# Local-attention layers on one core: the block transposes of the weights move ahead of the sums of squares on VectorE

## The reference

```
qkv = shift(x) @ Wqkv                        # half of the channels come from the token before
q = rope(q / max(|q|, 1e-12) * q_scale);  k = rope(k / max(|k|, 1e-12) * k_scale)
for each window of 32 queries:               # keys: its own window and the one before, 64
    sim  = q . k * 8, masked
    attn = softmax(sim)
    out  = attn @ v
x = out @ Wo + x
x = (a * gelu(gate)) @ W2 + b2 + x           # a, gate = LayerNorm(shift(x)) @ W1 + b1
```

## Time and profile before

| | us |
|---|---|
| median of 3 runs (lowest, highest) | 4337.44 (4333.52, 4338.48) |
| the profiled execution | 4332.56 |
| its span in the profile | 4330.7 |
| PE busy in the span | 3969.2 (92%) |
| DVE busy in the span | 3898.8 (90%) |
| POOL busy in the span | 2662.2 (61%) |
| ACT busy in the span | 2606.0 (60%) |

### The profile page before, as it was taken

The page is one execution under the profiler, slowest core; times in us unless marked ns, Lnnn a source line. Parts: engine busy times, 40 slices in busy tenths (PEclk is TensorE's granted clock), DMA queues, the critical chain, the costliest instruction groups (busy, mean ns, idle before and its releaser), DMA issues. The chain is left out here.

```text
span 4330.7 us, 124520 instructions
## 1 busy us (share of the span) xinstructions
PE 3969.2 (92%) x48616; PEld 2753.4 (64%) x48616; DVE 3898.8 (90%) x4863; ACT 2606.0 (60%) x3780; POOL 2662.2 (61%) x4596
## 2 busy tenths in 40 slices
PE   5988999898899999999999999999999999999996
PEld 3666666665566666666666666666666666666664
DVE  5777787786999999999999999999999999999994
ACT  3555555554456666666666666666666666666663
POOL 3545454453666666676766666667666667667673
PEclk9999999998999999999999999999999999999999
DMA  4444444443000001000010000100001000010000
GB/s 110 87 86 88 91 88 92 90 90 87 30 13 16 15 22 36 19 15 18 19 37 18 18 15 19 39 18 16 16 21 40 16 16 17 19 38 16 17 16 15
DMA packets 342517, 166.35 MB, mean 38 GB/s; under 512 B 114240, under 2 KB 337472, under 8 KB 341184
## 3 DMA queue, kind: packets, MB, share of 16 engines
q1 hardware_dynamic: 342208, 161.99, 16.6%
HBM read 115.67 MB, written 33.69 MB: 34 GB/s over the span
## 5 line engine op out<-in xcount | busy, mean ns | idle before, releaser
L616 POOL TENSOR_TENSOR pn<-es,rden 128x1024 f32<-128x1024 f32 x192 | 366.7, 1910 | 688.0 <-DVE rden L940 688.0
L707 ACT ACTIVATE y<-ps 128x1024 f32<-128x1024 f32 x384 | 372.3, 1021 | 507.1 <-PE ps L1169 507.1
L620 POOL TENSOR_TENSOR t<-t 128x1024 f32<-128x1024 f32 x192 | 454.7, 2368 | 88.0 <-DVE t L892 88.0
L664 ACT ACTIVATE t<-ps,amx 128x512 f32<-128x512 f32 x512 | 347.9, 689 | 251.5 <-DVE amx L812 251.5
L892 DVE TENSOR_TENSOR t<-ps,tabl 128x512 f32<-128x512 f32 x768 | 491.0, 681 | 0.0
L890 DVE TENSOR_TENSOR t<-ps,tabl 128x1024 f32<-128x1024 f32 x384 | 467.2, 1217 | 16.3 <-ACT sq L723 13.2
L812 DVE TENSOR_REDUCE amx<-ps 128x2 f32<-128x1024 f32 x256 | 311.6, 1217 | 180.3 <-PE ps L1049 178.9
L622 POOL TENSOR_TENSOR t<-t 128x1024 f32<-128x1024 f32 x192 | 453.0, 2359 | 2.3 <-DVE t L892 2.3
L994 DVE TENSOR_TENSOR qn<-t,rn 128x2048 f32<-128x2048 f32 x192 | 438.1, 2282 | 5.0 <-POOL rn L398 5.0
L950 DVE TENSOR_REDUCE ss<-sq 128x32 f32<-128x2048 f32 x192 | 437.0, 2276 | 0.0
L1024 PEld LDWEIGHTS ps<-cst,qn 128*128 128x128 f32 x3072 | 348.1, 141 | 112.2 <-issue 58.6
(11 more groups left out here) (135 smaller groups left out, 8256.7 us busy)
## 6 DMA issues: line engine op xcount, KB each, us to landing
y<-values_dram SPq DMA_DIRECT2D x128, 256.0 KB, 4.9
wm<-values_dram SPq DMA_DIRECT2D x128, 256.0 KB, 4.8
values_dram<-qT SPq DMA_DIRECT2D x64, 256.0 KB, 2.4
tokens_dram<-x SPq DMA_DIRECT2D x96, 128.0 KB
xs<-tokens_dram SPq DMA_DIRECT2D x192, 64.0 KB, 1.8
xw<-tokens_dram SPq DMA_DIRECT2D x192, 64.0 KB, 1.9
xsh<-x SPq DMA_DIRECT2D x48, 128.0 KB
xsh<-x SPq DMA_DIRECT2D x48, 127.0 KB
```

The source lines that it names most:

```text
L616: nc.gpsimd.tensor_tensor(heads(pn[:], H), heads(es[:], H), rden[:].unsqueeze(2).to_broadcast([P, H, KEYS]), ALU.mult).then_inc(l_p, 1)
L620: nc.gpsimd.tensor_tensor(t1[:, 0:INNER], t1[:, 0:INNER], t2[:, 0:INNER], ALU.add).then_inc(l_rotq, 1)
L707: return act.activation(y[:].rearrange("p h (w q) -> p w h q", w=NW)[:, 2 * half:2 * half + 2], src.rearrange("p (w h q) -> p w h q", w=2, ...
```

## The change

In VectorE's `turn`, the block transposes of the weights, with their two waits (for pn from POOL, `l_p`, and for the matrix product that read the old pT, `l_y`), move from behind L961 to a place straight behind the rope of the keys, ahead of the sums of squares (L950). All else stays.

```
@@ -947,6 +947,12 @@
                     rotate(0, u, pool3, l_rq)
                     dve.wait_ge(l_sqk, t + 4)
                     rotate(1, u, pool1, l_rk)
+                if s.has(1):
+                    dve.wait_ge(l_p, t + 2)
+                    past(dve, l_y, t + 1)
+                    nc.vector.transpose(pT[:].rearrange("p n h q -> p n h q"),
+                                        pn[:].rearrange("p (h n k) -> p n h k", h=H, n=2)).then_inc(l_pT, 1)
+                if s.has(3):
                     nc.vector.tensor_reduce(ss[:], heads(sq[:], 2 * H), X, ALU.add).then_inc(l_ss, 1)
                     dve.wait_ge(l_ss, t + 4)
                     nc.vector.tensor_tensor(ss[:], ss[:], floor_const[:], ALU.max).then_inc(l_fl, 1)
@@ -959,11 +965,6 @@
                     dve.wait_ge(l_o, t + 1)
                     xb = x[:, bass.ds((s.b * NU + c) * DIM, DIM)]
                     nc.vector.tensor_tensor(xb, xb, ps_o, ALU.add).then_inc(l_x, 1)
-                if s.has(1):
-                    dve.wait_ge(l_p, t + 2)
-                    past(dve, l_y, t + 1)
-                    nc.vector.transpose(pT[:].rearrange("p n h q -> p n h q"),
-                                        pn[:].rearrange("p (h n k) -> p n h k", h=H, n=2)).then_inc(l_pT, 1)
                 if c == 0 and s.ffn(2):
                     gate(s.f2, 2)
                 if c == 1 and s.ffn(2):
```

More of the change, by code:

```diff
@@ L961, in turn @@
                     nc.vector.tensor_tensor(xb, xb, ps_o, ALU.add).then_inc(l_x, 1)
[L962 to L966, removed]
                 if c == 0 and s.ffn(2):
```

## The result

The changed kernel took 4377.10 us in the median of 4 runs (4374.09 to 4380.31), the kernel before 4337.96 (4 runs, 4333.52 to 4342.20): ratio 1.009, 95% interval 1.0073 to 1.0108. The direction was right and the size wrong: 39 us where 78 were forecast, outside the range. The profiled execution took 4374.09 us, span 4372.3, 41.5 us over that of before.

A forecast was written before the change was run, and what follows sets the result against it. VectorE was taken to bound the plain turns, with GpSimd's Newton chain 0.36 us from binding. Terms of 60.8 + 7.5 - 3.2 + 4.6 + 4.7 + 2.7 + 1.4 = 78.5 us on the 4337.44 median gave 4416 us, range 4385 to 4445.

The forecast's parts named there:

- What is behind L954: GpSimd's Newton chain needs 4.15 us from L954 to L994; the move leaves 3.34 us of work there.
- So L954 comes 1.17 us later: Plain turns: the transposes, now ahead of L950, delay L954 by their full 1.17 us.
- anything that VectorE adds or waits for goes straight into the period: Plain turns, c = 2 and 3: VectorE has no idle time, so its added work or waits lengthen the turn fully.
- The stall of 0.81 us: VectorE's idle wait before L994 in plain turns, claimed for 75 turns: 60.8 us.
- The turns c = 0, value 0: The statistics leave 6.22 us from L954 to L994; less 1.17 still above 4.15, so no VectorE stall.
- L1169 and the two releases: With c = 0 TensorE's 1.68 us wait before L1169 passes from pT to x, keeping its length; value 0.
- The turns c = 1: L994 comes 0.42 us later, net 0.26 us in 29 turns: 7.5 us; L616 still precedes the transposes.
- The five turns at the end of a layer, +4.6 us: Five turns c = 1 have 4.41 us from L954 to L994 and lose 0.91 us each: 4.6 us.
- The transposes beside L622 cost nothing: The moved transposes run beside GpSimd's L622 without being held: 0, with 1.2 us a turn as far end.
- The faster one: Rival: the end of TensorE's pT wait with c = 0 decides, winning 19 us, giving 4318; chance 0.04.
- nothing: Rival: TensorE's 94% is the true pace and its backlog takes up a late L994; 4337, chance 0.05.
- GpSimd's takeover: Rival: with c = 1 all twelve LayerNorm operations slip behind L994, 1.12 us a batch, 4454; chance 0.11 including held transposes.

The follow-up runs named there:

- e1: Changed kernel with two Newton steps instead of three for the norms of q and k (eight GpSimd operations, not twelve): 4316.36 us, ratio 0.996 to the kernel before.
- e5: Kernel before with a fourth Newton step (16 GpSimd operations for 12), transposes in their old place: 4466.65 us, ratio 1.0306.
- e9: Kernel before with two of the sixteen heads left out of TensorE's output product: 4321.96 us, ratio 0.9972.
- e2: Kernel before with only the transposes moved ahead of the statistics, behind L954; L961 stays behind the statistics: 4334.61 us, ratio 1.0001.
- e3: Kernel before with L961 and the transposes both moved ahead of the statistics, behind L954: 4322.81 us, ratio 0.9979.
- e6: Kernel before with scale_tables (L876 and L880) moved one turn ahead, from c = 1 to c = 0: 4321.59 us, ratio 0.9977.
- e10: Changed kernel with two of the sixteen heads left out of TensorE's output product: 4382.57 us, ratio 1.012 to the kernel before.

## Why the prediction was right in its mechanism and wrong in its size

- *What is behind L954.* Right. 4.15 us from L954 to L994 as the filling turn had it; 118 waits for `rn`, 74.8 us, the commonest 0.68 or 0.69 us (55 of them). e1 takes the chain's excess away and the loss goes; e5 adds to the chain and a loss comes without the move.
- *"So L954 comes 1.17 us later"*, and with it *"anything that VectorE adds or waits for goes straight into the period"*. This is the step that failed. L954 came 0.98 us later, measured from L994. VectorE was not the pace of the plain turns: TensorE was, by 0.08 us (e9), and L622 held L952 for about another 0.10 (read from the rows; no run frees it by itself). Both had no row as idle time. The stall of 0.81 us was added to a turn of 15.49 that was VectorE's 15.3 plus waiting: 0.62 us came of it in c = 3, 0.47 in c = 2. Against the sum: -12 us in the plain turns.
- *The turns c = 0, value 0.* The stall is indeed not there, but the same two reserves are, and 0.09 us more between L910 and L961: -0.22 us in each, -10 us, where I had looked for a cost and not for a gain.
- *L1169 and the two releases.* Right: e2 gives 0, e3 the gain, though half of the 19 us. The sum of these waits was kept, as said, but 0.2 us a batch had gone from it and short waits in the plain turns had come in.
- *The turns with the bias.* They are in no term of the sum and came out at -2.8 us; the clock did that, by chance as far as is known.
- *The turns c = 1.* Right in each part: the fifth operation, L616 ahead of the transposes by 0.04 us, L958 held, +0.42 us from L994 to L994. That L616 still came first was partly luck: the prediction gave it 0.19 us to spare, and it had 0.04.
- *The five turns at the end of a layer, +4.6 us.* Wrong in sign: -9.3. I took their distance from L954 to L994 and did not look at the rest of the turn, where L876 and L880 stood behind GpSimd's passes; a delay of GpSimd by 1.1 us, which I had worked out for the turn c = 1, let them in first. The rows of both kernels show it, and e6 shows the same products short once they are away from the passes.
- *The transposes beside L622 cost nothing.* Right: 1.236 us in the mean, 1.238 before.
- *The rivals.* The faster one falls with e2, "nothing" with the measured time and e1. GpSimd's takeover did not come, since four operations of the chain were left ahead of L995, as counted.

## What to carry to other kernels

When two engines each seem full, take one engine's shortest distance between two of its instructions over all turns (here L994 to L938: 2.20, 2.28, 2.44 us) before you call it the pace; a wait shorter than the overlap of recorded neighbours has no row. A delay added to an engine that shares a path with another also changes who comes first at every later meeting, so read the whole turn, above all the rare ones, and not only the edge that the change moves. And move things into time in which the engine is held anyway, as the transposes with c = 1, not ahead of the start of a chain on which the same engine waits at its end.

## What the runs showed of the hardware

- The granted clock of TensorE fell after single waits of some 2 us in stretches that were busy else: 1.92 us of waiting, then 0.57 in the mean of 4 us (e10), while in the changed kernel 1.47 us at the same place left it at 1.00. The wait alone doesn't decide: in e10 the clock fell in 17 of the 47 turns c = 0, while waits of 1.9 us stand in about twice as many, and in e9 a wait of 2.14 us left it up in one turn, while behind ten others of this kind the turns were 1.6 us longer. Less work for TensorE thus made the changed kernel no faster: 13 turns lost 0.6 us each by it, and 0.2 in the turn behind.
- The Trainium skill (TensorE: Matmul & The Clock Gate, Part 1) has the clock depend on how busy TensorE has been of late. The rows of e10 agree in kind.
- VectorE's block transposes (one SBUF input) and GpSimd's passes over SBUF ran beside each other at full speed, 1.23 us each time, where VectorE's floor over 32 columns with two SBUF inputs took 1.20 us, held by the same pass (0.19 us where it is free).
